# A token-mixing and routed-LoRA FFN kernel: all columns by Strassen in four blocks of 290, instead of two of 448 and a plain 264

## The reference

```python
h = einsum('bct,bcd->bdt', x, weights[condition])      # 128 batches, 64x64 mixing matrix each
result = einsum('bnd,od->bno', h, W_base) + b_base      # 1024 -> 1024
logits = einsum('bnd,ed->bne', h, W_gate)               # 8 experts
top_p, top_i = top_k(softmax(logits), 2); top_p /= sum(top_p)
route_w = sum(one_hot(top_i, 8) * top_p[..., None], -2)
hw = einsum('bnd,erd->bner', h, A) * route_w[..., None]  # 8 experts, rank 16
out = x + result + einsum('bner,eor->bno', hw, B)
```

## Time and profile before

| | us |
|---|---|
| median of 3 runs (lowest, highest) | 952.94 (952.38, 955.5) |
| the profiled execution | 952.68 |
| its span, first to last instruction | 950.9 |
| PE / VectorE / ScalarE / GpSimd busy | 938.5 / 430.8 / 383.6 / 543.9 |

### The profile page before, as it was taken

How to read it: one execution, slowest core, us unless ns; L and a number is a source line. 1 busy time by engine, 2 the same in 40 slices (tenths; PEclk the granted TensorE clock), 3 DMA queues, 4 the chain that set the end, 5 groups by cost and what they waited for, 6 DMA issues and landing times.

```text
span 950.9 us, 16849 instructions
## 1 busy us (share of the span) xinstructions
PE 938.5 (99%) x5462; PEld 881.5 (93%) x5462; DVE 430.8 (45%) x1333; ACT 383.6 (40%) x815; POOL 543.9 (57%) x514
## 2 busy tenths in 40 slices
PE   8899999999999999999999999999999999999998
PEld 6789999999999999999999999999999999999997
DVE  5774444434444434444444444344444344443444
ACT  6644434333344334343333343343433433433332
POOL 2956466545565554665555755556655557555560
PEclk9999999999999999999999999999999999999999
DMA  9333322233322333223333223332223332233312
GB/s 315 119 100 134 119 98 86 105 121 132 110 85 97 109 128 126 95 87 101 121 132 110 95 92 109 122 132 88 91 96 121 132 110 98 90 110 121 132 46 87
DMA packets 41452, 107.13 MB, mean 113 GB/s; under 512 B 4449, under 2 KB 8674, under 8 KB 41442
## 3 DMA queue, kind: packets, MB, share of 16 engines
q1 hardware_dynamic: 41440, 107.01, 32.7%
q10 hardware_dynamic: 2, 0.00, 0.0%
HBM read 73.43 MB, written 33.55 MB: 113 GB/s over the span
## 4 chain that ended last, share of the span: by engine, by line
PE 93%; POOL 2%; DMA 1%; issue 1%; SPq 1%; ACT 1%; DVE 1%; POOLq 0%; DVEq 0%
PE ps L791 55%; PE ps_r L791 18%; PE ps_out L809 10%; PE ps_out L819 9%; DMA w_sum<-in_w_t 1%; PE ps_hwt L815 1%; POOL s_lo L312 1%; POOL a_lo L308 0%; POOL s_sum L333 0%; ACT w_hi L416 0%; POOL s_sum L319 0%; SPq L220 0%; POOL s_sum L325 0%; SPq L224 0%; SPq L230 0%
## 5 line engine op out<-in xcount | busy, mean ns | idle before, releaser
L308 POOL TENSOR_TENSOR a_lo<-raw,a_hi 128x512 fp32r<-128x512 f32 x128 | 164.7, 1307 | 239.5 <-ACT a_hi L400 239.5
L610 DVE TENSOR_TENSOR z_sum<-ps,z_sum 128x448 f32<-128x448 f32 x155 | 96.8, 625 | 242.1 <-PE ps L791 242.0
L791 PE MATMUL ps<-w_hi,s_hi 128*128 128x448 f32 x496 | 183.7, 370 | 0.4 <-DVE z_sum L610 0.4
L791 PE MATMUL ps<-w_lo,s_hi 128*128 128x448 f32 x496 | 181.2, 365 | 0.0
L791 PE MATMUL ps<-w_hi,s_lo 128*128 128x448 f32 x496 | 179.7, 362 | 0.0
L791 PE MATMUL ps<-w_hi,a_hi 128*128 128x448 f32 x372 | 138.9, 373 | 3.4 <-POOL a_lo L308 3.4
L791 PE MATMUL ps_r<-r_lo,a_hi 128*128 128x264 f32 x496 | 140.8, 284 | 0.0
L791 PE MATMUL ps_r<-r_hi,a_hi 128*128 128x264 f32 x496 | 140.7, 284 | 0.0
L791 PE MATMUL ps_r<-r_hi,a_lo 128*128 128x264 f32 x496 | 140.6, 283 | 0.0
L791 PE MATMUL ps<-w_lo,a_hi 128*128 128x448 f32 x372 | 135.7, 365 | 0.0
L791 PE MATMUL ps<-w_hi,a_lo 128*128 128x448 f32 x372 | 135.6, 364 | 0.0
(11 more groups left out here) (97 smaller groups left out, 1592.9 us busy)
## 6 DMA issues: line engine op xcount, KB each, us to landing
raw<-in_x_t SPq DMA_DIRECT2D x128, 256.0 KB, 2.9
o_sb<-in_x SPq DMA_DIRECT2D x64, 512.0 KB, 3.9
out_x<-o_sb SPq DMA_DIRECT2D x62, 512.0 KB, 2.6
w_sum<-in_w_t SPq DMA_DIRECT2D x8, 448.0 KB, 9.3
r_raw<-in_w_t SPq DMA_DIRECT2D x4, 264.0 KB, 4.3
table_raw<-in_cond_w SPq DMA_DIRECT2D x2, 256.0 KB, 9.1
b_raw<-in_b_t SPq DMA_DIRECT2D x1, 512.0 KB, 11.0
out_x<-o_sb SPq DMA_DIRECT2D x2, 224.0 KB, 2.1
```

The costliest lines, as they stand in the source:

```text
L308: pool.tensor_tensor(a_lo[j][:], raw[j][:], as_f32(a_hi[j][:]), ALU.subtract).then_inc(s_a_lo[j], 1)
L610: return dve.tensor_tensor(to, bank[:, 0:NS], other, ALU.add)
L791: mm = pe.matmul(bank[:, 0:w.shape[-1]], a[:, k, :], w[:, k, :], start=(opens and k == 0 and q == 0), stop=(closes and k == KH - 1 and q = ...
```

## The change

All 1160 columns go through Strassen. They are four blocks of NB = 290: block 0 holds 226 base columns and half of A, block 1 the other half of A, the gate and 218 base columns, blocks 2 and 3 are 290 base columns each. Blocks 0 and 2 form the left problem X, 1 and 3 form Y; each has seven products of twelve matmuls, 290 wide. Plain R goes. The products alternate between X and Y in two pairs of banks (`ps_a`, `ps_b`), and there are four output banks. The fourth also holds the transpose and the small expert rows, is not seeded, and its mix opens the accumulation after a wait for `s_hwt_lo`; GpSimd adds the bias of block 3 to x instead (`x_bias`). A21 is no longer split after pair 0. S4 and the rest keep their makers, in new orders. The last pair has an order of its own and stores in eight pieces. Below, the first `step` is GpSimd's and the second PE's.

```diff
-BASE_COLS = [312, 448, 264]
+BASE_COLS = [226, 218, 290, 290]
-WARM_UP = 10
+WARM_UP = 12
...
-        w_hi = sb("w_hi", [P, 7, KH, NS], F32R)
-        r_hi = sb("r_hi", [P, KT, width[R]], F32R)
+        w_hi = sb("w_hi", [P, 2, 7, KH, NB], F32R)
...
+        ps_a = [psum(f"ps_a{s}") for s in range(2)]
+        ps_b = [psum(f"ps_b{s}") for s in range(2)]
+        ps_bank = [psum(f"ps_out{c}") for c in range(4)]
+        ps_hwt = ps_bank[3][:, 0:P]
...
+            def x_bias(p, t):
+                pool.wait_ge(s_x_in[t], 16 * p + 16)
+                pool.tensor_tensor(o_sb[t][:, base(3)], o_sb[t][:, base(3)], bias[:, block_of(3)],
+                                   ALU.add).then_inc(s_x_bias[t], 1)
...
             def step(p, last):
-                a_rest(p, A21)
                 a_rest(p, A22)
-                pool.wait_ge(s_mixed[0][Q], p)
+                pool.wait_ge(s_mixed[0][1], blocks(p - 1, 3))
                 fetch_mix(p, 0)
+                if not last:
+                    a_rest(p + 1, A11)
...
                 fetch_mix(p, 1)
                 s_rest(p, 4, raw[A12][:], s2_hi, s2_lo)
+                x_bias(p, 0)
...
+                a_rest(p + 1, A12)
+                sum_s3(p + 1)
+                sum_s1(p + 1)
+                s_rest(p + 1, 3, s3[:], s3_hi, s3_lo)
+                sum_s2(p + 1)
+                sum_s4(p + 1)
+                s_rest(p + 1, 2, s2[:], s2_hi, s2_lo)
+                s_rest(p + 1, 1, s1[:], s1_hi, s1_lo)
+                x_bias(p, 1)
...
+            def mix_block(p, t, c, bank=None):
+                pe.wait_ge(s_z_lo[t][c // 2], blocks(p, c))
+                pe.wait_ge(s_mix[t], p + 1)
+                if c == 3 and bank is None:
+                    pe.wait_ge(s_hwt_lo, 2 * p + t + 1)
+                elif c == 2:
+                    pe.wait_ge(s_seed[1] if bank is None else s_seed_last, 2 * p + t + 1 if bank is None else 1)
+                elif c < 2:
+                    pe.wait_ge(s_seed[0], blocks(2 * p + t, c))
+                for q, (m, z) in enumerate(((0, z_hi(t, c)), (0, z_lo[t][:, c]), (1, z_hi(t, c)))):
+                    mm = pe.matmul(ps_out[c] if bank is None else bank[:, 0:NB], mix[t][:, m, :], z,
+                                   start=(c == 3 and q == 0), stop=(q == 2), skip_group_check=True)
+                mm.then_inc(s_mixed[t][c // 2], 1)
...
             def step(p, last):
                 pe.wait_ge(s_a_lo[A11], p + 1)
+                p1(p, X)
+                mix_block(p - 1, 1, 1)
+                p1(p, Y)
+                mix_block(p - 1, 1, 2)
                 pe.wait_ge(s_s_lo[2], p)
+                p6(p, X)
                 turn_hw(2 * p - 1)
+                p6(p, Y)
+                mix_block(p - 1, 1, 3)
+                pe.wait_ge(s_hwt_lo, 2 * p)
+                lora(1, 0)
+                lora(1, 1)
                 pe.wait_ge(s_a_lo[A12], p + 1)
+                p2(p, X)
+                lora(1, 2)
+                lora(1, 3)
+                p2(p, Y)
                 pe.wait_ge(s_s_lo[3], p)
+                p7(p, X)
+                mix_block(p, 0, 0)
+                p7(p, Y, lambda: mix_block(p, 0, 1))
+                if not last:
+                    pe.wait_ge(s_s_lo[1], p)
+                    p5(p, X)
+                    finish(p)
+                    return
...
+            def finish(p, first=False):
+                p5(p, Y, lambda: turn_hw(2 * p))
+                pe.wait_ge(s_s_lo[4], p)
+                p3(p, X)
+                pe.wait_ge(s_hwt_lo, 2 * p + 1)
+                lora(0, 0)
+                lora(0, 1)
+                p3(p, Y)
+                pe.wait_ge(s_a_lo[A22], p + 1)
...
+                p4(p, X)
+                mix_block(p, 0, 2)
+                lora(0, 2)
...
+                p4(p, Y)
+                mix_block(p, 0, 3)
+                lora(0, 3)
+                mix_block(p, 1, 0)
```

More of the change, by code:

```diff
@@ L52, in adaln_ffn @@
     PAIRS = TILES // 2
[L53 to L59, removed]
+    NB = COLS // 4
+    base_at = [sum(BASE_COLS[:c]) for c in range(4)]
+    H0_AT = BASE_COLS[0]
+    EH = ER // 2
+    base_in = [0, EH + E, 0, 0]
+    assert C == D == P // 2 and ER == P and E == 8 and sum(BASE_COLS) == O and H0_AT + EH == EH + E + BASE_COLS[1] == NB
     with ExitStack() as ctx:
@@ L95, in adaln_ffn @@
         mix = [sb(f"mix{t}", [P, 2, P], F32R) for t in range(2)]
[L96 to L100, removed]
+        z_hi_a = sb("z_hi0", [P, 2, NB], F32R)
+        z_hi_b = sb("z_hi1", [P, 4, NB], F32R)
+        z_sum, z_lo = zip(*[shared(f"z_sum{t}", f"z_lo{t}", [P, 4, NB]) for t in range(2)])
         top = sb("top", [P, 8])
@@ L149, in adaln_ffn @@
         s_t_lo = {t: sem(f"T{t}_lo_made") for t in (1, 2, 3, 4)}
+        s_first = [[sem(f"first_z{t}_{side}") for side in SIDES] for t in range(2)]
+        s_b12_used = [sem(f"B12{s}_used") for s in range(2)]
+        s_a11_used = sem("pair0_A11_used")
         s_raw_in = [sem(f"raw{j}_in") for j in range(4)]
@@ L173, in adaln_ffn @@
         s_mix = [sem(f"mix{t}_ready") for t in range(2)]
-        s_mixed = [[sem(f"mixed{t}{c}") for c in range(3)] for t in range(2)]
+        s_mixed = [[sem(f"mixed{t}_{side}") for side in SIDES] for t in range(2)]
         s_h = sem("h_copied")
@@ L517, in first @@
[L517 to L540 removed]
+                t_top(2, Y, T2)
@@ L614, in _, with add_u2, add_u3 @@
-            u3 = z_sum[1][:, cols(Q)]
+                return dve.tensor_tensor(to, bank[:, 0:NB], other, ALU.add)
+            p1 = [z_sum[1][:, s] for s in range(2)]
+            u2 = [z_sum[0][:, 2 + s] for s in range(2)]
+            u3 = [z_sum[1][:, 2 + s] for s in range(2)]
+            def add_u2(p, s):
+                dve.wait_ge(s_p1_out, upto(p, s))
+                dve.wait_ge(s_p[6], upto(p, s))
+                add(ps_b[s], p1[s], u2[s]).then_inc(s_u2, 1)
+            def add_u3(p, s):
+                dve.wait_ge(s_p[7], upto(p, s))
+                add(ps_b[s], p1[s], u3[s]).then_inc(s_u3, 1)
@@ L813, in turn_hw @@
             def turn_hw(i):
                 pe.wait_ge(s_hw, i + 1)
-                pe.transpose(ps_hwt[:, 0:P], hw[:], ident[:]).then_inc(s_hwt, 1)
-            def lora(t, c):
-                for q, (h, b) in enumerate(((hwt_hi, b_hi), (hwt_hi, b_lo), (hwt_lo, b_hi))):
-                    mm = pe.matmul(ps_out[c][:, 0:BASE_COLS[c]], h[:], b[:, base(c)], start=False,
-                                   stop=(q == 2), skip_group_check=True)
-                mm.then_inc(s_out_mm[t][c], 1)
+                source = last_hw if isinstance(i, int) and i == TILES - 1 else hw[:]
@@ new lines, in turn_hw, with lora @@
+                pe.transpose(ps_hwt, source, ident[:]).then_inc(s_hwt, 1)
+            def lora(t, c, bank=None, last=False):
+                h_hi, h_lo = (last_hwt_hi, last_hwt_lo) if last else (hwt_hi, hwt_lo)
+                to = base_of(ps_out[c] if bank is None else bank, c)
+                for q, (h, b) in enumerate(((h_hi, b_hi), (h_hi, b_lo), (h_lo, b_hi))):
+                    mm = pe.matmul(to, h[:], b[:, base(c)], start=False, stop=(q == 2), skip_group_check=True)
+                mm.then_inc(s_out_mm[t][c // 2], 1)
@@ L823, in _ @@
             pe.wait_ge(s_zeros, 1)
             for j in range(WARM_UP):
-                pe.matmul(ps_out[j % 3][:], zeros[:, 0:P], zeros[:], start=True, stop=True).then_inc(s_opened, 1)
-            def first_r(bank, t, half):
-                pe.wait_ge(s_a_lo[2 * t + half], 1)
-                for j in range(2):
-                    piece = 2 * half + j
-                    if t == 0:
-                        pe.wait_ge(s_r_lo, piece + 1)
-                    for k in range(2 * j, 2 * j + 2):
-                        a, w = 2 * t + half, half * KH + k
-                        for q, (u, v) in enumerate(((a_hi, r_hi), (a_hi, r_lo), (a_lo, r_hi))):
-                            mm = pe.matmul(bank[:, 0:width[R]], u[a][:, k, :], v[:, w, :],
-                                           start=(w == 0 and q == 0), stop=(w == KT - 1 and q == 2))
-                return mm
@@ L865, in _ @@
-            pe.wait_ge(s_z_lo[0][R], 1)
-            first_q(ps_r, 1, 0, "B12").then_inc(s_p[7], 1)
-            mix_chunk(0, 0, L)
-            first_q(ps_5, 0, 1, "B22").then_inc(s_p[3], 1)
-            mix_chunk(0, 0, R)
+            for s in range(2):
+                for t in range(2):
+                    first_product(t, 0, "B11", s)
+            for s in range(2):
+                for t in range(2):
+                    first_product(t, 1, "B21", s).then_inc(s_first[t][0], 1)
+            pe.wait_ge(s_z_lo[0][0], blocks(0, 0))
```

937 lines of the change are left out of this document (481 added, 456 removed).

## The result

The changed kernel takes 957.17 us (median of 10, 956.87 to 957.5) and the kernel before 953.1 on the same chip (median of 10, 952.16 to 955.5): ratio 1.0043, 95% interval 1.0035 to 1.0051. It is slower by 4 us, where 945.1, 8 faster, was forecast. The profiled execution has a span of 955.5 us against 950.9: 4.6 more.

What follows compares the result with a forecast made beforehand. Between start and tail, the number of TensorE matmuls times the spacing of their starts was taken as the bound. Steady pairs -6.0, start -2.3 and tail +0.5 summed to -7.8 us, giving 945.1, range 934 to 962.

Steps and rivals of the forecast that it cites:

- The start: Ahead of pair 2: stall and slow clock go, T work grows; -2.3 us in all, pair 2 at 71.8 instead of 74.1.
- The stall and the slow clock: At 40.59 us PE's 3.37 us wait for a_lo and the half speed behind it would go: -5.2 us.
- The bounds of the start: Start's -2.3 us to lie between -5.2 (written as nothing comes back) and +1 (all of VectorE's 5.0, plus 0.6).
- The steady pair: In the loop, 290s at 133.6 ns: a pair takes 28.81 us against 29.01, 6.0 us less over 30 pairs.
- Case C: Rival in the steady pairs: 290s spaced 135.3 to 136.6 ns, so slower, 956 to 964 us; chance 0.23.
- The narrow LoRA matmuls: In each steady pair, 12 matmuls of 226 and 218 columns at 0.112 us each: 1.34 us.
- E: Rival: narrow LoRA matmuls cost more than rows suggest; doubled from 0.112 to 0.224 they give 985 us; chance 0.05.
- D: Rival: new wait each pair, likeliest PE for hw at the transpose in p5(Y); 15 us more, 960; chance 0.14.
- VectorE, ScalarE, GpSimd in the pair: Added work beside TensorE in each steady pair fits under 28.8 us with half the time free; costed at nothing.
- The tail: After the last LoRA matmul, one more VectorE output and two more stores: +0.5 us, between -0.5 and +1.5.
- case A: The forecast's own case: 290s at 133.0 to 134.5 ns, no steady stall, 942 to 950 us; chance 0.40.

Runs made afterwards that it cites:

- the run of widths: Separate kernel computing nothing of the reference: 24 back-to-back matmuls at each of 19 widths, some again with other engines at work; 290 columns took 133.5 ns.
- before_a11_early: Kernel before, with GpSimd making lo of A11 ahead of the lo parts of S3 and S1, lo of A12 ahead of S1's; 955.06 us, ratio 1.0016.
- after_start_order: Changed kernel with the queues of the first pairs reordered on ScalarE, VectorE and TensorE, same work; 956.78 us, ratio 1.0038.

## Why the prediction was wrong, step by step

- **"The start"** is the step that failed: -2.3 forecast, +5.7 measured, 8.0 of the 12.4 us by which the span missed its forecast. With its -2.3 the kernel would have come out 3.4 us faster, not slower. It put VectorE's larger T work at its clean volume, +5.0, and let it hide behind PE. T came to +10.4 on VectorE, since its operations lie beside GpSimd's and take longer there (the timeline), and GpSimd's take longer beside them (the timeline, and the runs without T remainders or without T). And I laid VectorE's queue, which I had called "nearly full", beside PE's order and saw short waits; taking work away showed that each us of VectorE costs 0.4 of start. Another order of the same work brought 0.6, with 1.7 lost to the clock.
- **The stall and the slow clock:** that they would go was right. That this gives 5.2 us back was not: in the kernel before, moving GpSimd's a_lo alone made it slower by 2 us, and with the mix moved too 2.8 came back. That the 5.8 us of plain products which needed no T matrix also covered its making before is argued, not tested.
- **The bounds of the start:** -5.2 to +1 did not hold +5.7, because VectorE's term was bounded by its volume. The rows of VectorE before show little of the stretching (2168 ns beside 2058 for the same elements; 1798 and 1608 beside a clean 1360 now). GpSimd's rows at the start showed more, a sum of 2.88 us at 41.93, and were nowhere in the sum.
- **The steady pair:** the mechanism was right (matmuls times spacing, no wait), the size off. The spacing at 290 came out at 134.4 for 133.6: 204 x 0.8 = 0.16 us a pair, 5.0 us in all. Case C has the gain of columns used up from 134.8 on; by the forecast's own terms it is (29.01 - 1.56)/204 = 134.6, and the 0.034 that was left is what 134.4 gives. No neighbouring width could have told it better: at one width the spacing moves by more than that from program to program, and why is open.
- **The narrow LoRA matmuls:** 0.112 forecast, 0.109 measured; E is refuted: in the run of widths too nothing from 128 to 226 columns took more than 111.5.
- **D, a new wait each pair:** none. Transposes, the added banks and hwt_lo are covered as laid out.
- **VectorE, ScalarE, GpSimd in the pair:** 14.87, 11.34 and 17.59 busy against forecasts of 14.4, 12 and 17.2; off the path, as costed.
- **The tail:** -0.1 for +0.5.

That the range, 934 to 962, held 957.2 is luck: it reached there through case C, a spacing of 135.3 to 136.6, while the spacing measured lies in case A, whose own range ended at 950.

## What to carry to other kernels

When a change grows a preparation that runs while TensorE already works, add up each helper engine's queue over that stretch, and for VectorE and GpSimd add the two together where both read SBUF: here a nearly full VectorE cost 0.4 us of start for each us of work. Try orders as well, one at a time and on the chip: one gave 2.8 us, one 0.6, and one cost 2.8 of start, through a single wait behind which the clock fell. When a change trades fewer columns for more matmuls, measure the spacing at the new width in the kernel itself first: below about 240 columns a matmul here got no cheaper, and at 290 the spacing differed by up to 4.6 ns between programs and layouts.

## What was not expected of the hardware

- With these float32r operands 128, 160, 192, 218 and 226 columns all took 111 ns a matmul, 240 took 112.1.
- The spacing at one width is not one number: 290 columns between 131.9 and 136.5 ns, 448 between 202.5 and 206.5, each repeated to 0.2 ns within its run. With the operands at the same place 290 took 133.5 in one program and 136.5 in another. Another order of the PSUM banks changed nothing; moving the weights by 5152 bytes added 0.3 ns a matmul. What sets it stays open.
- VectorE's and GpSimd's operations stretch each other: 1.36 us to as much as 2.46 on VectorE, 1.29 to 3.09 and a 0.29 cast to 2.1 on GpSimd.
- In a wait of 6.98 us (before_a11_early) the granted clock fell to half, and TensorE ran at it for 5.1 us behind the wait. After waits of 2.50 us (after_start_order) and 3.37 us (the kernel before) it fell behind the wait, at 40.4 and 41.7 us, and came back at 43.8 and 45.1. Behind the warm-up, waits of up to 1.7 us left it at 1.00.
